# Five late layers of a graph network written as one program, with sums begun across layer boundaries

## The reference

```python
# block 0: edge MLP and sum over edges, then a node update      -> x1
# block 1: three SAGE convolutions, 128 -> 256 -> 48 -> 128     -> x2
#   conv(h) = (segment_sum(h[src]) / deg) @ Wl.T + h @ Wr.T + b   (relu between)
# block 2: three layers with l2 norms                            -> x3
for i in range(3):
    agg = l2norm(segment_sum(x[src], dst) / denom)
    out = agg @ Wl[i].T + bl[i] + l2norm(x) @ Wr[i].T
    x = relu(out) if i != 2 else out
# block 3: two graph convolutions with edge weights              -> out
h = relu(gcn(h, W1, b1)); x = x + gcn(h, W2, b2)   # msg = (h @ W)[src] * norm
```

## Time and profile before

| | |
|---|---|
| time, median of 3 runs | 2111.16 us (2110.62 to 2114.35) |
| profiled execution | time 2114.53 us, span 2113.0 us |
| mean granted TensorE clock | 0.784 |
| busy share: PE / DVE / ACT / POOL | 66% / 47% / 31% / 40% |
| PE in 1500 to 1550 us | 50.00 us busy, clock 1.00 |
| PE in 1550 to 1600 us | 39.56 us busy, clock 0.86 |
| DMA in 1800 to 1850 us | 389 GB/s |

### The profile page before, as it was taken

How to read it: one execution, slowest core, us unless ns; L and a number is a source line. 1 busy time by engine, 2 the same in 40 slices (tenths; PEclk the granted TensorE clock), 3 DMA queues, 4 the chain that set the end, 5 groups by cost and what they waited for, 6 DMA issues and landing times. The chain is left out here.

```text
span 2113.0 us, 31286 instructions
## 1 busy us (share of the span) xinstructions
PE 1404.5 (66%) x10748; PEld 931.7 (44%) x10748; DVE 1002.5 (47%) x2903; ACT 659.3 (31%) x1704; POOL 854.2 (40%) x876
## 2 busy tenths in 40 slices
PE   2416555555555555545565479887989896899997
PEld 1304444344444443333443245565555564455444
DVE  5576667676757575666776433124122234111101
ACT  1214444444444444444444201123233322000000
POOL 5027777777777777777777500000000000000001
PEclk8557676766666667676767589987989997999999
DMA  5525454545444545445545300001000002971770
GB/s 150 147 60 153 126 149 128 152 127 150 127 141 132 148 128 144 126 128 150 152 137 147 87 28 13 2 27 42 2 5 1 10 29 91 389 280 43 291 280 29
DMA packets 203430, 245.71 MB, mean 116 GB/s; under 512 B 36779, under 2 KB 177991, under 8 KB 203252
## 3 DMA queue, kind: packets, MB, share of 16 engines
q1 hardware_dynamic: 175172, 184.20, 27.6%
q0 software_dynamic: 28080, 59.18, 10.8%
HBM read 173.93 MB, written 55.93 MB: 109 GB/s over the span
## 5 line engine op out<-in xcount | busy, mean ns | idle before, releaser
L857 POOL DMA_INDIRECT arena<-dram_PHL,src_of x806 | 809.5, 1004 | 329.2 <-issue 243.0
L1169 PE MATMUL psum<-arena 128*128 128x512 f16 x404 | 174.5, 527 | 302.3 <-DMA arena<-dram_PHL,src_of 302.2
L1180 PE MATMUL psum<-arena 128*128 128x100 f16 x1568 | 193.5, 241 | 104.3 <-ACT aw_out L1095 94.6
L2445 POOL DMA_DIRECT2D parts_a<-dram_x x7 | 5.3, 761 | 608.0 <-POOLq L2643 585.3
L1180 PEld LDWEIGHTS psum<-arena 128*128 128x128 f16 x1568 | 169.5, 126 | 178.7 <-issue 132.3
L1164 PE MATMUL psum<-arena 128*128 128x128 f16 x1612 | 175.9, 275 | 106.7 <-DVE arena L889 58.3
L1082 ACT ACTIVATE arena<-psum 128x512 f16<-128x512 f32 x202 | 120.4, 596 | 352.7 <-PE psum L1169 352.5
L1164 PEld LDWEIGHTS psum<-arena 128*128 128x128 f16 x1612 | 139.0, 126 | 116.6 <-issue 115.3
L917 DVE SCALAR_TENSOR_TENSOR arena<-psum,arena 128x512 f16<-128x512 f32 x202 | 138.1, 684 | 103.8 <-ACT arena L1082 96.4
L1182 PE MATMUL psum<-arena 128*128 128x50 f16 x1568 | 187.4, 222 | 0.0
L1832 PE MATMUL psum<-arena,parts_b 128*128 128x512 fp8e4 (+5 forms) x875 | 174.8, 360 | 6.6 <-DMA narrow_fold<-ident 5.3
(11 more groups left out here) (353 smaller groups left out, 2286.2 us busy)
## 6 DMA issues: line engine op xcount, KB each, us to landing
arena<-dram_aw SPq DMA_DIRECT2D x7, 6400.0 KB, 20.3
dram_aw<-aw_out SPq DMA_DIRECT2D x196, 200.0 KB
arena<-dram_aw SPq DMA_DIRECT2D x3, 4800.0 KB, 16.2
arena<-in_ea_quads SPq DMA_DIRECT2D x51, 256.0 KB, 3.3
arena<-dram_rel SPq DMA_DIRECT2D x51, 256.0 KB
arena<-arena SPq DMA_DIRECT2D x408, 32.0 KB
arena<-dram_PHL,src_of POOLq DMA_INDIRECT x806
arena<-dram_aw SPq DMA_DIRECT2D x2, 4000.0 KB, 13.8
```

What stands on the lines that cost most here:

```text
L857: nc.gpsimd.indirect_dma_start(gathered_p[:, slot, k, :], None, d["PHL"], bass.IndirectOffsetOnAxis(ap=src_of[:, b:b + 1], axis=0)).then_i ...
L1169: done = nc.tensor.matmul(out, ident_h[:, :], gathered_p[:, g % NPG, 0:n, part * D:(part + 1) * D], start=False, stop=(part == 1))
L1180: nc.tensor.matmul(out, hot_lo[:, u, p, :], hot_key[:, u, p, 0:2].rearrange("p a k -> p (a k)"), start=True, stop=False)
```

## The change

`narrow_layer`, `out_layer`, `norm_layer` (three times) and `weighted_layers` become one function, `late_layers`, with one `nc.Block`. The barriers between them are gone; there is one behind `wide_layer` as before. What each queue does:

- TensorE: two PSUM banks for sums, in turn. At each layer start the first two sums are begun over the tiles of groups 0 to 5 (`begin_sum`), the first ahead of the previous layer's last tail, the second behind it; then both are ended with the last three tiles. Every sum waits per source group for `split[k - 1].done`. Inside a layer the order is "sum c, tail c - 1" up to sum 6, with tail 5 behind it.
- The bias of out: no product; VectorE adds rows of it to x.
- ScalarE and VectorE: the chains as before, in the new order (the last two groups' `give` behind the last sum's copy).
- At the end of the last norm layer: transposes 0 to 4 and products 0 to 2 of the weighted layers ahead of the last tail, the rest behind it.
- SyncE: all weights of narrow, out, the first norm layer and the weighted layers at the start, then x; weights of the next norm layers once their slot is free; two slabs behind the load of x of the last group. GpSimd loads the first slab at the start, into the slot that `adj` doesn't overlap.

```diff
-def narrow_layer(nc, new, d):
-def out_layer(nc, new, d):
-                            last = nc.tensor.matmul(psum[:, 3, at], L.ones[0:1, :], b[:, :], start=False, stop=True)
-def norm_layer(nc, new, d, number, layers):
...
+def late_layers(nc, new, d):
+    LL, SL = 5, SLABS
+    SUM_BANK, MORE = (0, 6), (5, 6)
...
+        def slot_of(n):
+            return (n + SL - 1) % SL
...
+        def await_input(eng, k, c):
+            if k:
+                eng.wait_ge(split[k - 1].done, c + 1)
...
+                # SyncE, behind the loads of all first weights and of out's x
+                for c in range(G):
+                    load_x(d["x2"], c, G + c)
+                    if c == G - 1:
+                        sp.wait_ge(summed, LL * G)
+                        load_slab(1)
+                        load_slab(2)
+                    store_x(d["x3"], c, G + c)
...
+                # GpSimd
+                j0, j1 = windows_of(order[0])
+                pool.dma_start(slab[:, slot_of(0), 0:j1 - j0, :], d["aw"][j0:j1].rearrange("j p k -> p j k")
+                               ).then_inc(first_slab_in, 16)
...
+                def sum_tiles(n, first_group, end_group):
+                    k, c = n // G, n % G
+                    parts = takes[k]
+                    first, end = columns_of(c)
+                    if first_group == 0 and n >= 2:
+                        pe.wait_ge(agg_sb, n - 1)
+                    for group in range(first_group, end_group):
+                        await_input(pe, k, group)
+                        for t in tiles_of(group):
+                            for q, (at, width) in enumerate(parts.taken):
+                                last = nc.tensor.matmul(
+                                    psum[0:width, SUM_BANK[n % 2], 0:end - first],
+                                    parts.flat[:, t * parts.block + at:t * parts.block + at + width],
+                                    adj[:, t * NCOL + first:t * NCOL + end], start=(t == 0 and q == 0),
+                                    stop=(t == NT - 1 and q == len(parts.taken) - 1))
+                    if end_group == G:
+                        last.then_inc(summed, 1)
...
+                # TensorE's order
+                for k in range(LL):
+                    n0 = k * G
+                    if k:
+                        begin_sum(n0)
+                        tail(n0 - 1)
+                        begin_sum(n0 + 1)
+                    end_sum(n0, begun=(k > 0))
+                    if OUT < k < LAST:
+                        weight_norms(k)
+                    end_sum(n0 + 1, begun=(k > 0))
+                    for c in range(2, G):
+                        tail(n0 + c - 2)
+                        end_sum(n0 + c, begun=False)
+                    tail(n0 + G - 2)
+                transposed(0)
+                for m in range(3):
+                    transposed(m + 1)
+                    product(m)
+                transposed(4)
+                tail(LL * G - 1)
+                product(3)
+                for m in range(4, G):
+                    if m + 1 < G:
+                        transposed(m + 1)
+                    product(m)
...
+                # ScalarE's order
+                for k in range(LL):
+                    n0 = k * G
+                    if k:
+                        give(n0 - 1)
+                    if k > OUT:
+                        head(k)
+                    sums_out(n0)
+                    sums_out(n0 + 1)
+                    for c in range(2, G):
+                        give(n0 + c - 2)
+                        sums_out(n0 + c)
+                    give(n0 + G - 2)
+                for m in range(5):
+                    copy_t(m)
+                give(LL * G - 1)
+                for m in range(5, G):
+                    copy_t(m)
...
+                def widen(n):                      # VectorE, out
+                    dve.wait_ge(x_in, 16 * (c + 1))
+                    link(nc.vector.tensor_tensor(x[:, 0:m], x[:, 0:m], rows, ALU.add))
+                    dve.wait_ge(u_psum, n + 1)
+                    link(nc.vector.tensor_tensor(x[:, 0:m], x[:, 0:m], psum[:, 3, 0:m * D].rearrange(
+                        "p (t f) -> p t f", f=D), ALU.add))
...
+                # VectorE's order at the end of the last norm layer
+                for m in range(3):
+                    scale(m)
+                combine_normed(LL * G - 1)
+                for m in range(3, G):
+                    scale(m)
```

More of the change, by code:

```diff
@@ L2077, in _ @@
                         cut(c - 1)
-def narrow_layer(nc, new, d):
+def late_layers(nc, new, d):
+    LL, SL = 5, SLABS
+    NARROW, OUT, LAST = 0, 1, LL - 1
+    SUM_BANK, MORE = (0, 6), (5, 6)
     with ExitStack() as ctx:
[L2083 to L2135, removed]
@@ L2138, in out_layer, with sb @@
-def out_layer(nc, new, d):
[L2140 to L2147, removed]
-        x_in, x_ready, x_stored, normed = L.new("x_in"), L.new("x_ready"), L.new("x_stored"), L.new("normed")
+        def sb(name, shape, dt):
+            return ctx.enter_context(nc.sbuf_tensor("late_" + name, shape, dt))
@@ new lines, in late_layers, with loaded @@
+        wide_hT = (spare_b[:, 0:one], spare_b[:, 2 * one:3 * one])
+        out = spare_a[:, 0:one].rearrange("p (t f) -> p t f", f=D)
+        kept = list(range(G - SL, G - 1))
+        order = list(range(G)) + kept + list(range(G - SL)) + [G - 1]
+        loads = [n for n in range(2 * G) if not G <= n < G + len(kept)]
+        def slot_of(n):
+            return (n + SL - 1) % SL
+        def loaded(n):
+            return sum(0 < m <= n and m % SL == n % SL for m in loads)
+        w_in = [sem(f"w_in{i}") for i in range(2)]
@@ new lines, in sum_from_dram @@
+                def sum_from_dram(n):
+                    k, c = n // G, n % G
+                    pe.wait_ge(h_copied, 2 * k + 2)
+                    pe.wait_ge(counts_in, 16 * (n + 1))
+                    if n >= 2:
+                        pe.wait_ge(agg_sb, n - 1)
+                    m, rows = windows_of(c)[1] - windows_of(c)[0], rows_of(k)
+                    for t in range(NT):
+                        last = nc.tensor.matmul(psum[0:rows, SUM_BANK[n % 2], 0:m * W], h_copy(d)[:, t, 0:rows],
+                                                slab[:, 0, 0:m, t * W:(t + 1) * W], start=(t == 0), stop=(t == NT - 1))
+                    last.then_inc(summed, 1)
@@ L2458, in transposed @@
                 def transposed(m):
+                    bank = (1, 7)[m % 2] if m < G else 1
                     if m < G:
-                        transpose_parts(nc, d, d["h_in"], pe, m, ht_psum, ht_sb, banks=(1, 4))
+                        parts = gives[LAST]
+                        pe.wait_ge(split[LAST].done, m + 1)
+                        if m == 0:
+                            pe.wait_ge(ht_sb, LAST * G)
+                        if m >= 2:
+                            pe.wait_ge(ht3_sb, m - 1)
+                        for i, t in enumerate(tiles_of(m)):
+                            for q, (at, width) in enumerate(parts.taken):
+                                last = nc.tensor.matmul(psum[:, bank, i * P:(i + 1) * P], parts.tiles[:, t, at:at + width],
+                                                        ident_b[:, :], start=(q == 0), stop=(q == len(parts.taken) - 1))
+                        last.then_inc(ht3_psum, 1)
```

667 lines of the change are left out of this document (350 added, 317 removed).

## The result

The changed kernel takes 2031.36 us, median of 4 runs (2029.84 to 2036.42), against 2112.07 (2110.62 to 2114.35, 4 runs): ratio 0.962, 95% interval 0.961 to 0.963. The forecast was 2031. Its profiled run has a span of 2029.3 us, a time of 2030.84 and a mean granted clock of 0.807.

What follows compares the result with a forecast made beforehand. TensorE was taken to bound the norm layers, with losses at layer boundaries. Savings of 2.5 + 7.2 + 25.6 + 15.8 + 23.3 + 5.8 = 80.2 us gave 2031 us off the median; 8-in-10 range 2018 to 2052.

Steps and rivals of the forecast that it cites:

- Bound: Norm layers: TensorE bounds them, with no hole between groups; boundaries cost through waits for the last group's chain and a barrier.
- Parts 1 and 2: Start of narrow: no wait for `fold`, -2.5 us; narrow itself: full-speed sums, fewer waits, one cold start, -7.2 us.
- Part 3: Out, up to norm 0's first product: VectorE's chain becomes the bound, 113.8 us falls to 88.2, -25.6 us.
- Part 4: Norm 0, to the next layer's first product: TensorE back to back, 101.9 us falls to 86.1, -15.8 us.
- Part 5: Norm 1 and 2, to the last sum's end: 167.6 us falls to 144.3, -23.3 us.
- Part 6: Last norm sum's end (T) to the first weighted sum: 35.8 us falls to 30, -5.8 us.
- A: Out: TensorE's clock is low for most of the layer and binds again; price 12 to 30 us; chance 12%.
- B: Boundaries: sixth groups' chains late, `fold` late, serial entry to weighted layers; 24 us at most, 12 likely; chance 10%.
- C: Inside the sums: each of 196 waits empties TensorE's pipeline, 84 us on top, 2115 us, slower; chance 3%.
- D: Boundaries: TensorE's own order leaves holes between begun and ended sums, so they give half, 40 us: 2071 us; chance 3%.

Runs made afterwards that it cites:

- the run with the late slab: Changed kernel with the weighted matrix's first slab loaded only after the last norm sum: 2233.58 us, ratio 0.964 to the kernel before, on another chip.
- The two-bank run: Changed kernel with the transposes of h going to PSUM banks 1 and 7 in turn: 2231.92 us, ratio 0.964 to the kernel before, on another chip.
- The entry run: Changed kernel with ScalarE and TensorE work reordered at the entry into the weighted layers: 2208.05 us, ratio 0.960 to the kernel before, on another chip.
- the run with all three edits: Changed kernel with squares awaited late, two banks for transposes of h, and reordered weighted entry: 2203.75 us, ratio 0.959 to the kernel before, on another chip.

## Why the prediction held, step by step

**Bound.** Right in the main. TensorE bounds the norm layers, and the boundaries were the larger loss; without begun sums and with the wait for the whole layer 47 of the 81 us come back. The claim that a norm layer has no hole inside was wrong (2.11 and 1.13 us in norm 0, above).

**Parts 1 and 2.** -2.3 and -8.2 for -2.5 and -7.2. In narrow the cold start cost 1.5 us instead of 2.05 (12.34 to the first product), and six tails 4.5 instead of 4.8. `fold` was issued at 1335.94, ahead of the slab at 1336.65, and landed in 1.8 us; the slab took 24.5. That part 1 took nothing for it came out, but the reason given, another queue, is not shown. `fold` had landed before the slab's data flowed (19 GB/s in 1337 to 1338, 369 from 1340 on). The run with the late slab shows what the slab does to SyncE's transfers, since it issues the same ones in the same order without it. `fold` took 1.8 us in both. The 64 KB of weights issued 3.8 us behind it (1339.70) took 9.9 us beside the slab and 2.4 without it, and the last weights 17.3 against 3.2. None of these were wanted soon. Had `fold` stood in that place, it would have landed at about 1349.6 (an estimate, 1339.70 + 9.9), and it is wanted at 1348.50. So the order of issue was luck.

**Part 3.** -26.5 for -25.6, and by the mechanism named: VectorE's chain binds out. VectorE adds the groups' products at these times in the changed kernel:

```profile
1389.77 0.69 DVE L2598 TENSOR_TENSOR parts_a<-parts_a,psum 128x512 f32<-128x512 f32 x1 [6.18 <-PE psum L2352]
1398.38 0.69 DVE L1581 TENSOR_TENSOR parts_b<-parts_b 128x512 f16<-128x512 f32 x1 [3.54 <-ACT trash L1572]
1399.83 0.69 DVE L2598 TENSOR_TENSOR parts_a<-parts_a,psum 128x512 f32<-128x512 f32 x1
...
1449.54 0.56 DVE L2598 TENSOR_TENSOR parts_a<-parts_a,psum 128x384 f32<-128x384 f32 x1 [4.99 <-PE psum L2352]
```

The first starts 14.4 us behind out's first sum (14.3 forecast); the steps are 10.1, 9.6, 8.0, 9.6, 8.0 (9.8, 9.7, 8.5, 9.7, 8.5). The 0.5 us for x did not show: it loaded while VectorE stood 3.54 us for the squares, and it did show once these were gone, until x had two buffers. The hole at the sixth group's tiles is 4.36 us (4 to 6). What shows the bound best is the same kernel's other two traces. Their clock fell behind other holes, yet the sixth group starts on VectorE 59.7, 59.9 and 59.7 us behind out's first sum, and O is 87.3, 87.1 and 87.4. So falls of the clock inside out were covered, as forecast. The steps are not where the gain lies, though: these five took 46.4 us before and 45.3 after. In the kernel before the sixth group starts 65.0 us behind out's first transpose, so 5.3 of the 26.5 us come ahead of it and 21.2 behind it, at the boundary. One detail was wrong: the holes in out stand before the transposes (these wait for ScalarE's copy of h out of their one bank), not before the products. The two-bank run shows no difference in time from this. Of the bias, moving it to VectorE was costed at 0.86 us a step and freeing TensorE; the run with the bias product shows the changed kernel 2.8 us better off in out with it on VectorE.

**Part 4.** 86.2 for 86.1. No cover failed: with a margin of 1 us at the sixth group no hole stands at either boundary between norm layers.

**Part 5.** 144.3 for 144.3. The waits inside the sums cost nothing that shows: the 226 us at full speed hold over a hundred of them.

**Part 6.** 30.4 for 30. The first weighted product came at T + 11.3 (11.4), held as forecast by ScalarE behind the cast, and the seventh transpose was waited for 5.04 us. The entry run confirms the cause by taking it away: 10.6 us earlier at the second weighted sum. One addition in the prediction is off: 17.0 + 2.0 + 6.9 is T + 25.9 and not 26.2; the seventh transpose came at T + 26.0.

**Rivals.** A: in the profiled execution the clock fell only with the hole of 2.85 us and, at the end, with that of 4.36. The rows below are stretches of the changed kernel: behind the hole that ends at 1398; in 1408 to 1410, at full clock this time (in the kernel before, the row has 0.51 without a hole); in and behind the hole that ends at 1426; and around the one that ends at 1444:

```profile
1398.00:1404.00 6.00, 5.48 (x16) 2.91 (x17) 4.84 (x17) 1.14 (x3) 0.00 (x0) 0.50 0.16 48
1408.00:1410.00 2.00, 1.71 (x14) 1.28 (x13) 1.81 (x4) 1.12 (x2) 0.00 (x0) 1.00 0.00 0
...
1424.00:1426.00 2.00, 0.00 (x0) 0.00 (x0) 0.33 (x1) 1.91 (x9) 0.00 (x0) 1.00 0.23 70
1426.00:1428.00 2.00, 1.73 (x14) 1.59 (x15) 1.90 (x5) 0.70 (x2) 0.00 (x0) 1.00 0.00 0
...
1442.00:1448.00 6.00, 3.99 (x11) 1.98 (x12) 1.25 (x2) 1.09 (x6) 0.00 (x0) 0.50 0.02 5
```

B: neither `fold` nor a sixth group's chain was late in the norm layers; the serial entry was in the forecast already. C: refuted by part 5. D: refuted by the two layers at 86 us. The range of 2018 to 2052 was wider than needed: parts 4 and 5, half of the saving, were sums of rows at one clock, and came out to 0.2 us. That the whole is off by only 0.5 (80.7 for 80.2 by the medians) is in part luck, since parts 2 and 3 are off by 1.0 and 0.9 us.

## What to carry to other kernels

Read each layer to its end for holes, not its first groups alone. Where each step reads all of the step before, a barrier's price is mostly the bare chain of the last piece, not the barrier; releasing by pieces and beginning the next sum over what is there removes it. Another piece of work should stand between the last two tails. Once that is done, find the engine whose chain is now the longest and write its recurrence; here it gave the stretch to 1 us. If two engines bind at nearly the same step, relieving one of them gains little by itself. Then take its waits off one at a time: each one removed (the squares) uncovers the next (x), so a step's gain is less than the wait it removes until the last is gone.

## What the runs showed of the hardware

- A hole of one length had two outcomes, in one and the same kernel. Behind out's second group the changed kernel stood 2.85 us in the profiled execution and 2.84 in another, with the same instructions ahead of it. The first came back at a granted clock of 0.50 for 6 us (its four tiles' transposes take 0.63 us), the second at 1.00 (0.40 us):

```profile
1588.68 0.40 PE L2273 MATMUL psum<-ident_b,parts_a 128*96 128x128 bf16 x4 [2.84 <-ACT late_hT L2464]
```

- Neither did length sort them elsewhere. A hole of 2.51 us left 1.00, and in the run with all three edits one of 2.89 us at 1597 left 1.00 while one of 2.93 at 1613 brought 0.57 over 1612 to 1620. One of only 2.11 us brought 0.59 over 1556 to 1560 in the kernel before. The Trainium skill's "TensorE: Matmul & The Clock Gate", Part 1, says that the gate follows how busy the engine has been of late. The falls behind holes agree with that; the two outcomes behind one hole do not follow from that sentence alone. A price of 2 us for each hole, as I had considered, was too high for two of the changed kernel's four holes of over 1 us.
- A 6.4 MB load on GpSimd's queue left TensorE at full speed: with 369 to 397 GB/s over 1340 to 1344 the granted clock was 1.00, and a sum of 512 columns took 5.56 us (5.60 without it). Small transfers on SyncE's queue were slow beside it: the same twelve behind `fold` took 3.5 to 17.3 us by the medians, against 1.8 to 3.3 in the run with the late slab.
- The bias product, of one row, costs 0.6 us a tile at full clock: three fp32 products take 1.05 us a tile, two take 0.45 (1594.56 to 1596.35 in the kernel before with the bias on VectorE, four tiles).
